# Window attention and Laplacian merge on one core: whole q and k through an fp32 transform, column halves, and the Laplacian on GpSimd

## What is computed

```python
    # layer 0, on g = groupnorm(x)
    qk = einsum(g, QK_w) + QK_b;  v = einsum(g, V_w) + V_b
    # windows of 8x8 tokens, 6 heads, q scaled by HD ** -0.5
    o = irfft2(rfft2(qp) * rfft2(kp), s=(8, 8))
    attn = softmax(einsum("bhnd,bhmd->bhnm", o, vv) + bias[None])
    y = einsum("bhnm,bhmd->bhnd", attn, vv)
    x = x + (einsum("bchw,oc->bohw", y, proj_w) + proj_b)
    # layer 1, on g = groupnorm(x)
    edges = depthwise_conv3x3(g, [[0,-1,0],[-1,4,-1],[0,-1,0]])
    x = x + (conv1x1(g + edges, merge_w) + merge_b)
```

## Time and profile before

| | us |
|---|---|
| median of 3 runs | 5973.95 |
| lowest, highest | 5973.53, 5978.52 |
| the profiled execution, its own time | 5977.56 |
| its span | 5975.8 |
| PE busy, share of the span | 5684.8, 95% |
| DVE busy | 5053.2, 85% |
| ACT busy | 3167.7, 53% |
| POOL busy | 1995.5, 33% |

### The profile page before, as it was taken

One profiled execution on the slowest core, in us unless ns is written; L12 is line 12 of the kernel. 1 busy time (PEld: TensorE's weight loads), 2 busy tenths in 40 slices (PEclk: granted clock), 3 DMA queues, 4 the chain that ended last, 5 costly groups with the idle time before them and its releaser, 6 DMA issues.

```text
span 5975.8 us, 206127 instructions
## 1 busy us (share of the span) xinstructions
PE 5684.8 (95%) x91660; PEld 5026.7 (84%) x91660; DVE 5053.2 (85%) x8286; ACT 3167.7 (53%) x6020; POOL 1995.5 (33%) x1286
## 2 busy tenths in 40 slices
PE   7999999999999999999999999999999999999987
PEld 5888888888888888888888888888888888888876
DVE  4777788888889889888888888888888888888876
ACT  2666655555555555555555555555555555555531
POOL 0333333333333333333333333333333333333310
PEclk9999999999999999999999999999999999999999
DMA  4222133323333233332333333333233332222336
GB/s 132 68 63 59 55 79 102 103 79 94 96 106 102 81 92 102 98 99 81 96 102 106 91 82 95 105 104 90 83 101 100 103 85 77 78 78 81 83 90 163
DMA packets 392631, 550.56 MB, mean 92 GB/s; under 512 B 24838, under 2 KB 284873, under 8 KB 391754
## 3 DMA queue, kind: packets, MB, share of 16 engines
q1 hardware_dynamic: 391756, 537.37, 32.1%
HBM read 335.95 MB, written 201.33 MB: 90 GB/s over the span
## 4 chain that ended last, share of the span: by engine, by line
PE 66%; DVE 22%; ACT 9%; issue 2%; DMA 1%; SPq 0%; DVEq 0%
PE b_q L515 20%; PE b_s L621 7%; PE b_t L604 6%; PE b_q L590 5%; PE b_t L580 5%; DVE qkl L907 4%; PE b_s L523 4%; PE b_s L520 3%; ACT qkh L973 3%; PE b_t L562 3%; DVE late L768 2%; PE b_s L466 2%; DVE late L791 2%; DVE ssum L938 2%; ACT probs L1037 2%
## 5 line engine op out<-in xcount | busy, mean ns | idle before, releaser
L1080 POOL TENSOR_TENSOR probs<-probs,srec 128x768 f32<-128x768 f32 x512 | 880.7, 1720 | 2219.5 <-DVE srec L956 2219.5
L1069 POOL TENSOR_TENSOR probs<-probs,smax 128x768 f32<-128x768 f32 x512 | 754.1, 1473 | 1438.3 <-DVE smax L918 1438.3
L973 ACT ACTIVATE vs<-b_q 128x192 f32<-128x192 f32 x1024 | 338.6, 331 | 1360.5 <-PE b_q L515 1360.5
L913 DVE TENSOR_TENSOR probs<-b_s,posb 128x768 f32<-128x768 f32 x512 | 487.9, 953 | 578.5 <-PE b_s L621 578.0
L515 PE MATMUL b_q<-wnh,xh 128*128 128x288 f32 x2048 | 703.3, 343 | 66.7 <-DVE qkl L907 65.4
L907 DVE TENSOR_TENSOR qkl<-b_q,qkh 128x384 fp32r<-128x384 f32 x1024 | 566.0, 553 | 175.5 <-ACT qkh L973 141.3
L523 PEld LDWEIGHTS b_s<-yT,wp 128*128 128x128 f32 x4096 | 618.6, 191 | 53.0
L523 PE MATMUL b_s<-yT,wp 128*128 128x128 f32 x4096 | 622.5, 275 | 0.0
L520 PE MATMUL b_s<-yT,wp 128*128 128x256 f32 x2048 | 613.6, 381 | 2.1 <-DVE probs L913 1.6
L515 PE MATMUL b_q<-wnl,xh 128*128 128x288 f32 x2048 | 606.3, 296 | 0.0
L515 PE MATMUL b_q<-wnh,xl 128*128 128x288 f32 x2048 | 606.1, 296 | 0.0
(11 more groups left out here) (152 smaller groups left out, 13242.6 us busy)
## 6 DMA issues: line engine op xcount, KB each, us to landing
ld<-in_x SPq DMA_DIRECT2D x192, 512.0 KB, 4.9
late<-x_dram SPq DMA_DIRECT2D x112, 640.0 KB, 5.1
xs<-in_x SPq DMA_DIRECT2D x128, 512.0 KB, 5.6
x_dram<-late SPq DMA_DIRECT2D x128, 512.0 KB, 2.8
out<-late SPq DMA_DIRECT2D x128, 512.0 KB
late<-x_dram SPq DMA_DIRECT2D x240, 192.0 KB, 5.7
xs<-in_x SPq DMA_DIRECT2D x128, 256.0 KB, 5.9
x_dram<-late SPq DMA_DIRECT2D x128, 256.0 KB, 3.7
```

What stands on the lines that cost most here:

```text
L913: V.tensor_tensor(scored(i).rearrange("p (t q) m -> p t q m", q=4), scores.rearrange("p (t q m) -> p t q m", q=4, m=N), posb[:, :, :].unsq ...
L973: return A.activation(o, i, ACT.Copy)
L1069: P.tensor_tensor(probs[:, i % 2, :, :], probs[:, i % 2, :, :], smax[:, i % 2, :].unsqueeze(2).broadcast_to([128, 12, N]), ALU.subtract).t ...
L1080: P.tensor_tensor(probs[:, i % 2, :, :], probs[:, i % 2, :, :], srec[:, i % 2, :].unsqueeze(2).broadcast_to([128, 12, N]), ALU.mult).then_ ...
```

## The change

Five edits in one:

- `high` and `remainders` go. ScalarE copies q and k whole into `qk` (fp32), and the forward transform is four fp32 matmuls in place of eight float32r ones. The waits for `lo_out` become waits for `qk_out`.
- The second projection and pieces 4 and 5 lose their blocks of zeros: where a 128x128 stationary tile was half zeros, two 64-column tiles write the two halves of the output partitions (`out_rows`). The projection's output then takes 128 columns in place of 256, and VectorE adds it in three instructions in place of two.
- The Laplacian moves: `5x` to ScalarE (`centre`), the additions and two subtractions to GpSimd (`diagonal`, `neighbours`). In the last image's strips units 0 and 2 are made by VectorE (`late_stencil`). `border` runs only in strips 0, 1, 2 and 15 of an image.
- The heads are reordered (`HEADS`) so that `vT` has 384 columns in place of 512; the fourth transpose of v has 64 columns.
- At the start the first image's mean, spread and biases come at `m` 56, 58, 60 and after the last step.

```diff
             def project_b():
+                o = b_r[:, 256:384]
+                for i in range(2):
+                    out_rows = slice(i * CB, (i + 1) * CB)
+                    mm(o[out_rows], wp[:, 1, out_rows], yT[:, i, :, :].rearrange("p w (r c) -> p r w c", c=WS),
+                       start=True, stop=False, skip_group_check=True)
+                mm(o, wp[:, 4, :], rest, start=False, stop=True, skip_group_check=True).then_inc(proj_mm, 1)
...
-                    mm(o, mats(par, 1), za[:, k, at:at + 256], start=True, stop=False)
-                    mm(o, mats(par, 2), za[:, k, 512 + at:512 + at + 256], start=False, stop=False)
-                    mm(o, mats(par, 5), zb[:, k, at:at + 256], start=False, stop=True).then_inc(m_mm, 1)
+                    for half in range(2):
+                        out_rows = slice(half * CB, (half + 1) * CB)
+                        mm(o[out_rows], mats(par, 1)[:, out_rows], za[:, k, half * 512 + at:half * 512 + at + 256],
+                           start=True, stop=False, skip_group_check=True)
+                    mm(o, mats(par, 4), zb[:, k, at:at + 256], start=False, stop=True,
+                       skip_group_check=True).then_inc(m_mm, 1)
...
-                        for k, xx in enumerate((qkh, qkl)):
-                            for win in range(2):
-                                rows = slice(win * N, (win + 1) * N)
-                                last = mm(q_banks[0:NF, 2 * i + win, 0:QK], fwdh[rows, :], xx[rows, i, :],
-                                          start=(k == 0), stop=(k == 1))
+                        for win in range(2):
+                            rows = slice(win * N, (win + 1) * N)
+                            last = mm(q_banks[0:NF, 2 * i + win, 0:QK], fwd[rows, :], qk[rows, i, :],
+                                      start=True, stop=True)
...
-            def high(i):
+            def qk_copy(i):
                 act.wait_ge(qkv_mm, i + 1)
-                copy(qkh[:, i % 2, :], q_out).then_inc(hi_out, 1)
+                copy(qk[:, i % 2, :], q_out).then_inc(qk_out, 1)
+            def centre(v, unit):
+                src, r, zz = unit_views(v, unit)
+                if unit == 0:
+                    act.wait_ge(src_in[v % 3], 48 * (v // 3 + 1))
+                    if v >= 2:
+                        act.wait_ge(m_mm, m_count[8 * (v - 2 + MERGE_LAG) + PIECES - 1])
+                A.activation(zz, src[:, r + 1:r + 5, 1:W + 1], ACT.Copy, scale=5.0).then_inc(five_done, 1)
...
+            def neighbours(v, unit, half):
...
+                if half == 0:
+                    pool.wait_ge(diag_done, n)
+                    pool.wait_ge(five_done, 3 * v + unit + 1)
+                    P.tensor_tensor(zz, zz, d[:, 0:4, 0:W], ALU.subtract).then_inc(nb_done, 1)
+                else:
+                    pool.wait_ge(nb_done, n)
+                    P.tensor_tensor(zz, zz, d[:, 1:5, 1:W + 1], ALU.subtract).then_inc(z_done, 1)
```

More of the change, by code:

```diff
@@ L270, in program @@
             a_count[it] = a_count[it - 1] + (m_task(it) is not None and by_act)
+        border_count = list(itertools.accumulate(int(v % NS < 3 or v % NS == NS - 1) for v in range(STRIPS)))
         def m_region(it):
@@ L280, in m_wait, with stencil_unit, by_vector, pool_units @@
                 eng.wait_ge(a_read, a_count[it])
+        units = ((src_a, 0, za, 0), (src_b, 0, zb, 0), (src_a, 4, za, 512))
+        def stencil_unit(j):
+            blk, ph = divmod(2 * j, 8)
+            v = blk - STENCIL_LAG
+            return (v, ph // 2) if 0 <= v < STRIPS and ph < 6 else None
+        LATE = STRIPS - NS
+        def by_vector(v, unit):
+            return v >= LATE and unit != 1
+        def pool_units(v, unit):
+            return 3 * v + unit + 1 if v < LATE else 3 * LATE + v - LATE + (unit > 0)
+        def vector_units(v, unit):
+            return 2 * (v - LATE) + 1 + unit // 2
+        def unit_views(v, unit):
+            src, r, z, at = units[unit]
+            return src[v % 3], r, z[:, v % 2, at:at + 512].rearrange("p (r c) -> p r c", c=W)
         def doubles():
@@ L444, in _ @@
             last.then_inc(pos_mm, 1)
+            pe.wait_ge(m_read, 3)
+            bias(0, 1)
             def channels(field, width):
@@ L467, in piece @@
                     at = p % 2 * 256
-                    last = mm(o, mats(par, 3 + p // 2), zb[:, k, at:at + 256], start=False, stop=not alone)
+                    last = mm(o, mats(par, 2 + p // 2), zb[:, k, at:at + 256], start=False, stop=not alone)
                     if alone:
@@ L549, in _ @@
                     pe.wait_ge(v_out, 2 * j + 2)
+                    at = 2 * j % 8
                     for i in range(2):
-                        for t in range(2):
-                            last = nc.tensor.transpose(vt_out[:, i, t, :],
-                                                       vs[:, (2 * j + i) % 8, t * N:t * N + 128], ident[:, :])
-                    last.then_inc(vT_mm, 1)
+                        nc.tensor.transpose(vt_out[:, i, :], vs[:, at + i, 0:CA], ident[:, :])
+                    nc.tensor.transpose(vt_out[:, 2, :], vs[:, at + 1, CB:C], ident[:, :])
+                    nc.tensor.transpose(vt_out[0:CB, 2, :], vs[:, at, CA:C], ident[:, :]).then_inc(vT_mm, 1)
                 if pair(3):
@@ L581, in _ @@
                                           vs[rows, (2 * k + i) % 8, h * HD:(h + 1) * HD],
-                                          probsT[rows, i, h, :], start=True, stop=True)
+                                          probsT[rows, i, HEADS.index(h), :], start=True, stop=True)
                     last.then_inc(y_mm, 1)
@@ L929, in _ @@
                 m_result(2 * j)
-                edges(2 * j)
                 norms(2 * j)
-                if pair(0):
-                    remainders(2 * j + 1)
-                edges(2 * j + 1)
+                unit = stencil_unit(j - 1)
+                if unit and by_vector(*unit):
+                    late_stencil(*unit)
                 if pair(2):
@@ L1028, in _ @@
                     v_copy(2 * j)
-                    high(2 * j)
+                    qk_copy(2 * j)
                 split(h, 0 if j % 2 == 0 else 2)
@@ L1055, in _ @@
                     copy(osb[:, :, :].rearrange("p k n -> p (k n)"), o_out_ps).then_inc(o_out, 1)
+                if stencil_unit(j):
+                    centre(*stencil_unit(j))
                 if pair(0):
@@ L1076, in _ @@
                                     ).then_inc(xl_done, 1)
+                if unit:
+                    neighbours(*unit, 1)
                 if pair(2):
@@ L1090 @@
     x = a["x"]
+    qk = np.concatenate([part * C + h * HD + np.arange(HD) for part in range(2) for h in HEADS])
     arrays = {
         "x": x,
-        "wqkvT": np.concatenate([a["L0_conv_QK_w"], a["L0_conv_V_w"]]).T,
-        "qkvb": np.concatenate([a["L0_conv_QK_b"], a["L0_conv_V_b"]])[None],
+        "wqkvT": np.concatenate([a["L0_conv_QK_w"][qk], a["L0_conv_V_w"]]).T,
+        "qkvb": np.concatenate([a["L0_conv_QK_b"][qk], a["L0_conv_V_b"]])[None],
         "proj": proj_blocks(a["L0_conv_proj_w"]),
```

209 lines of the change are left out of this document (98 added, 111 removed).

## The result

The changed kernel takes **6072.84 us** (median of 4 runs, 6068.45 to 6079.79) against 5973.74 before (4 runs): ratio 1.0167, 95% interval 1.0151 to 1.0183. The prediction was 6000 with a range of 5895 to 6095: the sign was right and the time lies in the range, but the loss is 99 us where 27 were worked out.

What follows compares the result with a forecast made beforehand. PE's own work was taken to bound the doubles with pieces, the chain from the scores the one without. Steady strips, first part, start, boundaries and end: 22 + 11 - 2 - 8 + 4 = +27, about 6000 us, range 5895 to 6095.

Steps and rivals of the forecast that it cites:

- The transform: Forward transform on PE: four fp32 matmuls in place of float32r ones add .60 us a double.
- rival 4: Forward transform: row halves don't overlap in fp32, +660 us, 6660 us in all; chance .03.
- Column halves: Second projection and pieces 4 and 5: 64-column tiles cost .34 us a visit, saving .10 net each, .60 a strip.
- Rival 1: The six visits a strip to 64-column tiles: changing column tiles costs little, 5895 or 5778 us; chance .15.
- Waits of A and B: PE's waits of .77 us in the double with pieces 0 and 1 and .47 with pieces 2 and 3 both go.
- D: The double without a piece, bound by the chain from scores through exponential to `y`: +.14 us, to 9.9.
- C: The double with pieces 4 and 5, bound by PE's own work: +.30 us, to 11.9.
- Rivals 2 and 3: 2: GpSimd late without pieces, 109 us per further us, chance .12; 3: both piece waits stay, 135 us, chance .06.
- VectorE at 3400 us: VectorE's busy time falls from 5053 to about 3400 us without remainders and Laplacian.
- The first failed step: Image boundaries: means and spreads wait less for VectorE's backlog, -8 us over 7 images (0 to -20).
- The second failed step: Strips after the loop, set by VectorE's last unit: +.2 us each, 17 strips, +4 (-30 to +15).
- First part: The first 76 doubles, which have no pieces: +.14 us each, +11 us.

Runs made afterwards that it cites:

- e9: The changed kernel with the second projection alone in full-width tiles, three matmuls of 128 columns; pieces 4 and 5 keep 64-column tiles: 6032.51 us.
- e1: The changed kernel with all the Laplacian's additions and subtractions back on VectorE, 5x staying on ScalarE: 6091.17 us.
- e2: The changed kernel with the float32r forward transform and VectorE's remainders back, everything else as changed: 5897.49 us.
- e5: The changed kernel with GpSimd's Laplacian operations cut to a few elements in six of each image's sixteen blocks, around the boundaries: 6033.21 us.
- e11: The changed kernel with six filling matmuls a strip after the loop and GpSimd's unit 1 there cut to a few elements: 6037.81 us.
- e3: The changed kernel with all three Laplacian units of a strip on VectorE after the loop, unit 1 no longer on GpSimd: 6084.31 us.
- e4: The changed kernel with eight extra fp32 matmuls ahead of piece 0 of each strip after the loop, filling TensorE's wait: 6049.20 us.
- e7: The changed kernel with the first image's mean, spread and biases at their earlier steps of the position bias, as before: 6075.44 us.
- e6: The changed kernel with full-width tiles, with blocks of zeros, for the second projection and pieces 4 and 5: 6042.39 us.

## Why the prediction was right or wrong, point by point

**The transform: right.** 1.49 a double against .90, +.59 for +.60. The two fp32 windows do run side by side; rival 4 is out.

**Column halves: right in the total.** Streaming is .43 and the projection takes .69, with .09 in the row ahead: .35 a visit for the .34 taken from the earlier trace rows. Rival 1 is out. The bound of .18 had been read closely: by the printed starts 1.40 less three times .43 leaves .11, which would make .22; nothing hung on it. The Trainium skill, TensorEngine Tiling (Array Packing), section Key Properties, says that changing the tiling mode drains the TensorE; the trace agrees for column tiles, by the .35 a visit. What the prediction did not see is that the output can be narrowed without halving the tile, and that this is cheaper (e9: 40 us).

**Waits of A and B, and D: right.** Both waits are gone, D takes 9.93 for 9.9, A, B and C 11.27, 11.27 and 11.96 for 11.3, 11.3 and 11.9. e1 and e2 show that either edit alone would have removed the waits. GpSimd's second operation is no bound in D: it ends 1.4 us after the scores (1.2 forecast), and GpSimd then idles 1.6 before the subtraction (1.8 forecast). Its busy time is 3328 us for about 3200, since a unit's three operations take 1.59 + 1.19 + 1.20 instead of 3.2, in 352 units. Rivals 2 and 3 are out in the steady state. The sign "PE's waits for VectorE under 30 us" did not hold: they fell from 210 to 111 us, and most of what is left lies at the start, at the boundaries and after the loop.

**VectorE at 3400 us: wrong, 3926.** The four rows add up to 1540, which gives 3513, not 3400. And the step took the rows' durations off the busy time. In a full queue they overlap (in the changed kernel's boundary step L723 begins at 2053.58, while L722, begun at 2052.44, is listed with 1.22), so less leaves than their sum: worked out from the trace of before, VectorE without these four lines is busy for 3711 us. The projection's output in three instructions (+118 us) and two units in each strip of the last image (+80) came on top, and `border` took some off. It did not matter for the time.

**The first failed step: "Means and spreads at image boundaries wait for VectorE's backlog: 7 images, -8 together".** Measured +35. It counted what VectorE is relieved of, and not that what is left to it there meets GpSimd at work. The rest of the term comes out as forecast: with GpSimd's Laplacian out of the way (e5) a boundary costs 9.7 instead of 11.1, six times, -8. The term put at nothing is the meeting, 7.3 us a boundary in e5, +44 in six. The step on GpSimd had named such exclusion and ended "few such pairs are left after the move, and the sum stays"; it looked at the steady step, where that is so (L937 keeps .95), and not at the boundary, where VectorE has casts, scalings and subtractions within SBUF. The trace of before had a sign of it: L688 met GpSimd's multiplication in seven of eight cases and took 1.22 or 1.62 us, and .46 in the one that met none. The page cited there (the Trainium skill, SBUF — State Buffer, section Who interferes with whom) also lists copy, cast and `tensor_scalar`, which can use the port pair shared with GpSimd, beside operations with two SBUF inputs; read to its end, it covers L718, L723, L724 and L727. The trace agrees: 1.30, 1.48, 1.12 and 1.11 us on average, where e5 has .45 and .46 for L723 and L724 and .75 for L727, while the reduction L937 and the additions out of PSUM (L915, .96) keep their time.

**The second failed step: the part after the loop, "about +.2, 17 strips, +4 (-30 to +15)".** Measured +36. What is left for the order is .26 a strip (e11), for the .2 of the prediction. Two terms were missing: .62 a strip, because L850 falls beside GpSimd's L1098 (e3, e11), and the clock, 24 us (e4). The prediction has no term for the clock. Its mean was .996 before, but two of 16 strips after the loop had already fallen to .86 with a wait of 2.44 us; what a wait of 3.48 does was not asked. The same term is in the boundary: of the 5.5 us by which its longest step exceeds a steady C, 2.5 are the wait and about 3 the lower clock after it; at the other five boundaries the step exceeds it by 4.0 to 4.3, with 1.7 for the clock.

**Smaller terms.** Start -10.6 for -2, of which the order of the steps is no more than 5 (e7) and the missing remainders some 4 in doubles 0 to 3 (e2: 40.0). First part +4.7 for +11. Last image +8 for 0: of the 1.24 a strip that the prediction takes off, .57 was not there to lose, as 43.63 before would have shown (the wait at piece 0 was missing, those for VectorE's remainder and result were there).

**The sum.** Predicted 27, measured 98.5 in the profiled executions: start and first part -6, steady strips +25, boundaries +35, last image +8, after the loop +36. That the sign was right is the steady state's doing; that the time fell inside the range is the width of the range, which was meant for rivals 1 and 2, and neither of them happened as described.

## What to carry to other kernels

Work that is moved to a second engine is free only where nothing on the critical path meets it: look at the rare steps (boundaries, the part behind the loop) as closely as at the steady one, and at each operation that the other engine still has there. Where TensorE waits, ask what the longer wait does to its granted clock; matmuls that only fill the wait can pay for themselves (24 us in e4). And price the edits of a change apart: here one edit of five (fp32 operands, +.60 a double) hid a gain of 1.25%.

## What the runs showed of the hardware that was not expected

- VectorE and GpSimd in SBUF hold each other up for about as long as the other's instruction still runs: an addition of 128x645 takes .82 alone and 1.44 when GpSimd had begun first, a cast of 64x576 .45 and up to 1.83, and GpSimd's multiplication 1.97 instead of 1.48 when VectorE's L960 has just begun (in half of the steps, before and after).
- After a wait of 2.53 us the granted clock was .50 for the next six us; after the loop, with a wait of 3.48 in each strip, it stayed full in some strips and fell in others. Why in some only was not settled; with the wait filled it stayed full in all.
- Entering 64-column tiles from full ones costs .09 us even in the row ahead of them: the transposes to L557 take .75 from start to start, and .66 when L555 of e6, in full tiles, follows.
